# A two-expert-layer kernel: 71 blocks of rows in place of 72, and three of sixteen one-hots on GpSimd

## The reference, cut to what matters

```python
gate_logits = xs @ Wg                                  # 8192 x 8
weights, sel = jax.lax.top_k(gate_logits, 2)
weights = jax.nn.softmax(weights, axis=1)
h = relu(einsum('td,edf->etf', xs, W1) + b1[:, None, :])
out_e = einsum('etf,efd->etd', h, W2) + b2[:, None, :]
out = einsum('tk,tkd->td', weights, out_e[sel, tok[:, None]])
```

## Time and profile before

| | us |
|---|---|
| median of 3 runs | 2251.55 (2251.38 to 2252.23) |
| the profiled execution | 2256.53 |
| its span | 2254.7 |
| ffn1 one-hots | 708.59 to 751.12 |
| ffn2 one-hots | 1763.87 to 1806.42 |
| ffn1 block results, first to last | 782.8 to 1015.6 |

### The profile page before, as it was taken

How to read it: one execution, slowest core, us unless ns; L and a number is a source line. 1 busy time by engine, 2 the same in 40 slices (tenths; PEclk the granted TensorE clock), 3 DMA queues, 4 the chain that set the end, 5 groups by cost and what they waited for, 6 DMA issues and landing times. The chain is left out here.

```text
span 2254.7 us, 51777 instructions
## 1 busy us (share of the span) xinstructions
PE 1673.6 (74%) x16844; PEld 1360.7 (60%) x16844; DVE 1794.9 (80%) x4769; ACT 1480.4 (66%) x3849; POOL 1335.4 (59%) x1497
## 2 busy tenths in 40 slices
PE   5778777787654599993899999999987469997000
PEld 2555555455552388882788888888877258886000
DVE  6999999999878677785899999999957957776221
ACT  5787878788544577771788888888873747775000
POOL 3555556565500355533899999999870045553774
PEclk8888888888756699995999999999985679998555
DMA  1001010010340033331111111111102013333322
GB/s 35 15 15 29 15 29 21 22 29 10 95 146 19 27 81 80 82 72 33 26 29 31 31 30 31 31 31 31 27 8 75 0 49 80 81 82 64 80 77 56
DMA packets 145827, 101.59 MB, mean 45 GB/s; under 512 B 22144, under 2 KB 134688, under 8 KB 145568
## 3 DMA queue, kind: packets, MB, share of 16 engines
q1 hardware_dynamic: 110880, 54.20, 8.7%
q0 software_dynamic: 17408, 35.69, 6.9%
q10 hardware_dynamic: 17280, 8.40, 1.3%
HBM read 53.63 MB, written 35.65 MB: 40 GB/s over the span
## 5 line engine op out<-in xcount | busy, mean ns | idle before, releaser
L1067 POOL DMA_INDIRECT ffn_xs<-normed,ffn_tokeni x288 | 274.2, 952 | 450.6 <-DVE posi L1444 252.5
L1854 POOL TENSOR_TENSOR att_pl<-att_p,att_ph 128x384 f16<-128x384 f32 x512 | 454.6, 916 | 53.6 <-ACT att_ph L2075 45.3
L326 POOL TENSOR_TENSOR sq<-states,qS 128x256 f32<-128x256 f32 x256 | 243.0, 949 | 236.9 <-DVE states L754 235.0
L573 ACT ACTIVATE decayed<-states,alpha 128x64 f32<-128x64 f32 x1024 | 272.1, 336 | 107.4 <-DVE states L754 105.4
L1274 ACT ACTIVATE ffn_h<-bank,b_cols 128x256 f32<-128x256 f32 x576 | 226.1, 474 | 129.6 <-PE bank L1162 118.7
L2182 DVE TENSOR_REDUCE att_mx<-bank 128x3 f32<-128x384 f32 x512 | 279.6, 551 | 36.3 <-PE bank L1911 32.5
L2072 ACT ACTIVATE att_p<-bank 128x384 f32<-128x384 f32 x512 | 252.0, 492 | 57.1 <-PE bank L1948 54.3
L403 PEld LDWEIGHTS bank<-sq,ident 128*128 128x128 f32 x1024 | 225.6, 251 | 46.0 <-issue 26.7
L2075 ACT ACTIVATE att_ph<-bank 128x384 f16<-128x384 f32 x512 | 253.3, 495 | 0.0
L403 PE MATMUL bank<-sq,ident 128*128 128x128 f32 x1024 | 247.7, 413 | 3.3 <-POOL sq L326 3.3
L1175 PE MATMUL bank<-w_h,ffn_hh 128*128 x1152 | 226.0, 224 | 12.7 <-issue 3.8
(11 more groups left out here) (340 smaller groups left out, 5057.8 us busy)
## 6 DMA issues: line engine op xcount, KB each, us to landing
slots<-ffn_ys SPq DMA_DIRECT2D x144, 128.0 KB
normed<-ffn_xn ACTq DMA_DIRECT2D x32, 256.0 KB, 2.3
att_qz<-att_qp SPq DMA_DIRECT2D x256, 32.0 KB
ffn_xs<-normed,ffn_tokeni POOLq DMA_INDIRECT x288
xin<-in_x SPq DMA_DIRECT2D x64, 64.0 KB, 2.0
xres<-in_x SPq DMA_DIRECT2D x64, 64.0 KB, 2.0
x<-x SPq DMA_DIRECT2D x64, 64.0 KB, 1.8
x_all<-x SPq DMA_DIRECT2D x8, 512.0 KB, 4.8
```

The lines of the kernel that those rows point to most:

```text
L326: nc.gpsimd.tensor_tensor(sq[:, t, :].rearrange("p (h i j) -> p h i j", h=HL, i=D), states[:, t, :].rearrange("p (h i j) -> p h i j", h=HL ...
L573: ins = nc.scalar.activation(decayed[:, 64 * h:64 * h + 64], states[:, (t - 1) % TC, 64 * h:64 * h + 64], ACT.Copy, scale=alpha[p][:, t, h ...
L1067: pool.indirect_dma_start(xs[j % AHEAD][:, r, :], None, A["normed"], bass.IndirectOffsetOnAxis(ap=tokeni[:, BR * j + r:BR * j + r + 1], ax ...
L1854: nc.gpsimd.tensor_tensor(pl[:, h % RP, :], p32[:, h % RP, :], ph[:, h % RP, :], ALU.subtract).then_inc(low_done, 1)
```

## The change

Two edits. First, the number of blocks that are worked off becomes `NJ` = `NB` - 1 = 71; `quads` runs over 71 turns, the last turn of buffer 3 falls away (`turns(3)` is 17), the waits that counted 72 // 4 = 18 turns count `turns(p)`, and the HBM tensor `slots` has 71 x 256 rows. Second, in the one-hot stage ACT's `is_tile` does tile 7 only, and POOL makes the `isa` of tiles 5 and 6 and the `isb` of tile 5. A step's one-hots are then 7 `isb` and 5 `isa` on DVE, 1 `isa` on ACT, 1 `isb` and 2 `isa` on POOL. ACT's L1252 also waits for the new semaphore `pool_onehots`.

```diff
+NJ = NB - 1
...
-ACT_TILES = (6, 7)
+ACT_TILES = (7,)
+POOL_TILES = (5, 6)
+POOL_COLS = (5,)
...
-            for i in range(NB // AHEAD):
-                for p in range(AHEAD):
-                    step(i, p, i % 2)
+            for j in range(NJ):
+                step(j // AHEAD, j % AHEAD, j // AHEAD % 2)
+        def turns(p):
+            return len(range(p, NJ, AHEAD))
...
+            pool.wait_ge(route, R["col"])
+            def onehot(i, p):
+                u = 2 * i + p
+                if u >= OH:
+                    pool.wait_ge(counted, u - OH + 1)
+                for q in POOL_TILES:
+                    t = u * TQ + q
+                    if q in POOL_COLS:
+                        pool.tensor_scalar(isb[u % OH][:, q, :], X.slot_col[:, :], col_of[:, t:t + 1], None, ALU.is_equal)
+                    ins = pool.tensor_scalar(isa[u % OH][:, q, 0, :], X.slot_tile[:, :], tile_of[:, t:t + 1],
+                                             X.nth[:, t:t + 1], ALU.is_equal, ALU.mult)
+                ins.then_inc(pool_onehots, 1)
+            pairs(pool, 2 * NT // TQ, onehot)
...
-            for j in range(NB - AHEAD):
+            for j in range(NJ - AHEAD):
...
-                pe.wait_ge(fetched[p], before + 32 * (i + 1))
+                pe.wait_ge(fetched[p], 32 * (turns(p) * calls + i + 1))
...
+                act.wait_ge(pool_onehots, u + 1)
                 nc.scalar.activation(isa[u % OH][:, :, 1, :], isa[u % OH][:, :, 0, :], ACT.Copy, scale=X.row[:, :]).then_inc(rowed, 1)
...
-                    ins = v.tensor_scalar(isb[u % OH][:, q, :], X.slot_col[:, :], col_of[:, at], None, ALU.is_equal)
-                    if q not in ACT_TILES:
+                    if q not in POOL_COLS:
+                        ins = v.tensor_scalar(isb[u % OH][:, q, :], X.slot_col[:, :], col_of[:, at], None, ALU.is_equal)
+                    if q not in ACT_TILES + POOL_TILES:
...
-    A["slots"] = nc.dram_tensor("slots", (NS, E), F32).ap()
+    A["slots"] = nc.dram_tensor("slots", (NJ * BS, E), F32).ap()
```

More of the change, by code:

```diff
@@ L966, in ffn @@
         stats_seen = sem("stats_seen")
+        pool_onehots = sem("pool_onehots")
         x_part = [sem(f"x_part{k}") for k in range(8)]
@@ L969, in ffn @@
         xn_kept = [sem(f"xn_kept{p}") for p in range(2)]
-        fetched, before = X.fetched, 32 * (NB // AHEAD) * X.calls
+        fetched, calls = X.fetched, X.calls
         X.calls += 1
@@ L1021, in within @@
         def within(i, p, n):
-            return not isinstance(i, int) or AHEAD * i + p + n < NB
+            return not isinstance(i, int) or AHEAD * i + p + n < NJ
         def last_group(i, p):
@@ L1051, in _ @@
             for k in range(AHEAD):
-                sp.wait_ge(kept[k], 16 * (NB // AHEAD))
+                sp.wait_ge(kept[k], 16 * turns(k))
             if dst is None:
@@ L1068, in fetch @@
                         ap=tokeni[:, BR * j + r:BR * j + r + 1], axis=0)).then_inc(fetched[j % AHEAD], 16)
+            pool.wait_ge(route, R["col"])
+            tile_of, col_of = (x[:, :, :].rearrange("p k t -> p (k t)") for x in (tile, col))
+            def onehot(i, p):
[10 more added lines that the diff above has]
+            pairs(pool, 2 * NT // TQ, onehot)
             for p in range(2):
@@ L1082, in _ @@
             for p in range(AHEAD):
-                pool.wait_ge(kept[p], 16 * (NB // AHEAD))
+                pool.wait_ge(kept[p], 16 * turns(p))
             for g in range(NG):
@@ L1193, in _ @@
             quads(pe, step)
-            down(NB // AHEAD - 1, AHEAD - 1, expert(pe, regs, (NB // AHEAD - 1) % 2, AHEAD - 1))
+            last = (NJ - 1) // AHEAD, (NJ - 1) % AHEAD
+            down(*last, expert(pe, regs, last[0] % 2, last[1]))
         @block.scalar
@@ L1491, in _ @@
             quads(dve, step)
-            rows(NB // AHEAD - 1, AHEAD - 1, expert(dve, regs, (NB // AHEAD - 1) % 2, AHEAD - 1))
+            last = (NJ - 1) // AHEAD, (NJ - 1) % AHEAD
+            rows(*last, expert(dve, regs, last[0] % 2, last[1]))
             for g in range(0 if dst is None else NG):
```

## The result

| | before, us | after, us |
|---|---|---|
| median, four runs of each | 2251.62 | 2239.89 |
| ratio, with its 95% interval | | 0.995 (0.9937 to 0.9962) |
| the profiled execution | 2256.53 | 2241.95 |
| one-hot stage (start of `ffn_col` to start of `ffn_past`), ffn1 / ffn2 | 42.8 / 42.9 | 39.8 / 39.8 |
| block results, first to last, ffn1 / ffn2 | 232.8 / 232.4 | 225.3 / 226.7 |

The kernel became 11.7 us faster; 8 us slower was forecast.

What follows compares the result with a forecast made beforehand. DVE, with ACT level, was taken to bound the one-hot stage and PE the blocks. Blocks -6.5 and one-hots +14.4 (POOL's price outweighing DVE's saving) made +8 on the median 2251.55, so 2259.5 us, range 2232 to 2273.

Steps and rivals of the forecast that it cites:

- What bounds the kernel: DVE sets the one-hot stage, with ACT level; PE bounds the block stage; each us of the one-hot stage is the kernel's.
- One block less, -6.5: Block loops of ffn1 and ffn2: one middle block's period goes in each, 3.28 + 3.26 = -6.5 us.
- DVE loses 0.389: One-hot stage: DVE drops one `isb` and one `isa`, step 2.66 to 2.27, giving -12.4 us without a price.
- ACT loses 0.71: One-hot stage: ACT drops one `is_tile`, 0.40 of Abs and 0.31 of Relu, its round going from 2.70 to 1.99.
- POOL's length, 0.35: One-hot stage: a POOL one-hot takes 0.35 us, between 0.31 and 0.47, so three fit in a step at 1.05.
- the second rival: One-hot stage: POOL becomes the bound at 0.92 a one-hot, step 4.44, total 2302; chance 0.12, shared with a higher price.
- The price, 0.79 x 0.35 = 0.28 a one-hot: One-hot stage: each POOL one-hot costs DVE 0.28 us (0.22 to 0.39), step 3.11, turning the term into +14.4 us.
- The share of 0.72 to 0.83: Rows before the change: DVE's loss beside a POOL instruction, as share of POOL's own length; mean 0.79 applied to one-hots.
- the first rival: One-hot stage: POOL's one-hots cost DVE under 0.15 each; 2232.6 at 0, 2242 at 0.10; chance 0.37.

Runs made afterwards that it cites:

- the one-hots alone: Kernel before with only the new one-hot split, still 72 blocks: 2166.96 against 2171.68 us, ratio 0.9975.
- the spare one-hots: Kernel before plus three POOL one-hots a step that nobody reads, DVE and ACT keeping all work: 2179.61 against 2171.68 us, ratio 1.0031.
- the long one: Kernel before plus one spare POOL compare of 128x512 f16 a step, one scalar per partition: 2185.68 against 2172.48 us.
- two tensors on DVE and the spare one-hots: Kernel before with each DVE `isb` a two-tensor compare, plus three spare POOL one-hots a step: 2183.4 us, kernel before 2174.59.
- the spare sums: Kernel before plus three spare POOL two-tensor sums of 128x144 f16 a step: 2189.82 us in one run, kernel before 2174.59.
- The blocks alone: Kernel after with POOL's one-hots given back to DVE and ACT, leaving only the 71 blocks: 2163.82 against 2171.68 us, ratio 0.9961.
- the `isa` alone: Kernel after with POOL's `isb` given back to DVE, so POOL makes two `isa` a step: 2162.75 against 2171.68 us, ratio 0.9957.
- the split with two `isb`: Kernel after with POOL making two `isb` and one `isa` a step: 2248.48 us against 2259.89 for the kernel before, ratio 0.9951.

## Why the prediction was wrong

*What bounds the kernel: right.* DVE set the one-hot stage, and a us of it was a us of the kernel: in the one-hots alone the stages lost 6.3 and the kernel 4.7, in the spare one-hots they gained 7.4 and the kernel 7.9, in the long one 13.6 and 13.2. It was less close in two single runs: 12.1 and 8.8 with two tensors on DVE and the spare one-hots, 18.7 and 15.2 with the spare sums.

*One block less, -6.5: right.* The blocks alone gave -7.9 with 5.6 to 11.5, for two blocks of 2.89. In the first pair of traces the stretch of results shrank more, by 7.5 and 5.7, which is more than a block each, because the results also stood 0.06 and 0.03 closer. This is not the change's doing: with 71 and with 72 blocks they stood 2.89 apart in one series, and in a later trace of the kernel after 228.9 / 70 = 3.27.

*DVE loses 0.389: right. ACT loses 0.71: a little too much.* DVE's undisturbed distances are unchanged, and the step came out as 2.27 plus what POOL costs. ACT's busy time fell by 9.5 us a stage, 0.59 a step; it has 8 us of slack, so this changed nothing.

*POOL's length, 0.35: mis-sized.* It took 0.65 and 0.93, outside 0.31 to 0.47. The forecast took 292 ns of another single-input instruction as the nearest row and left the second rival's 0.92 as a far bound, because "no row is as slow for so few elements". No row had POOL compare at all. The condition of that rival, over 0.76 of mean length, was in fact met (0.83), but its time was not: it held DVE for 0.79 of POOL's round, where the round of 2.46 is simply level with DVE's. It costs little: with the price alone DVE would need 2.45.

*The price, 0.79 x 0.35 = 0.28 a one-hot: this is the step that failed, and it turned the sign.* Measured are 0.077 beside the full DVE load, 0.09 for the `isa` alone, 0.04 in the split with two `isb`, and (2.48 - 2.29) / 3 = 0.065 in the kernel after (39.75 / 16 = 2.48, and 42.85 / 16 - 0.389 = 2.29). As a share of POOL's length this is 5 to 10%. The share of 0.72 to 0.83 was read rightly for what it was, mostly POOL products of two tensors; the failed inference was to carry it to a compare, on the ground that DVE's L2147 had been held too. It had been, but by a POOL memset:

```profile
1033.70 4.50 DVE L2147 TENSOR_SCALAR att_xn<-x_all,att_mv,att_rstd 128x128 f32<-128x128 f32 x2 [3.09 <-ACT att_rstd L2042]
...
1034.22 3.83 POOL L1824 MEMSET att_qz<- 128x4096 f16 x1
```

The pair takes 0.60 at 1042.24, so 3.9 were lost, about the memset's length. So the row does show that a DVE instruction with one tensor can be held, but it says nothing of a POOL compare. With the two-tensor sum on POOL DVE is in fact held to the end of each, and the price is 46% of its length only because one short DVE instruction is let through each time; that is much more than a compare's, and still below the forecast's share. The swap on DVE's side shows that two tensors there do not bring the large price. Which property of POOL's instruction decides is open: the memset reads no tensor and stopped DVE the longest, and the sum differs from the compare in its operation too.

With measured terms the forecast's own sum would have been -6.5 - 12.4 + 96 x 0.065 = -12.7, against -11.7. That is the first rival, "POOL's one-hots slip in between", at the 0.10 or below for which it gave 2242; it had been given 0.37. Of its two reasons both are seen: most of a short POOL one-hot's length stops nothing, and a DVE instruction can make part of a hold good (731.22 in the kernel after, the second hold of the long one).

The Trainium skill (SBUF — State Buffer, Who interferes with whom) has the shared port pair as an exclusive lock that is held for the full instruction. By that, were POOL the first each time, DVE would have stood still for 2.5 us of each step and the stage would have been (2.27 + 2.5) x 16 = 76 us, an estimate; it was 39.8. For this pair of instructions the measurement decides against the rule; for POOL's two-tensor sum, at whose end the DVE instruction beside it ends too, and for the memset of 3.83 that cost 3.9 the trace agrees with it.

## What to carry to other kernels

Before work is moved to GpSimd beside a busy VectorE, put the same instructions there as spare work, with nobody reading them: one such run gives both their length and their price to VectorE. The price does not follow from the length: it was 0.018 to 0.09 us for compares of 0.6 to 1.15 us, 0.195 for a sum of 0.425 and 0.43 for a compare of 1.63. A price that rows show for two-tensor products, or for a memset, must not be carried to compares. When a share of work is moved, the aim is that both engines are level; here the moved work made GpSimd level with VectorE at 2.46 us a step, and only giving some of its long instructions to a third engine with slack brought the rest.

## What was not expected of the hardware

- A compare on GpSimd with 128 f16 elements and one scalar per partition takes 0.64 us, with 144 elements and two such scalars 0.93, with 144 and two fixed numbers 0.72, with 512 elements and one scalar 1.63. A sum of 144 f16 elements with two tensor inputs takes 0.425 and so is the faster form, though the dearer one for VectorE, which gets one instruction done per sum.
- Which engine stands still depends on both kinds. With VectorE's two-tensor compares in the stage, each GpSimd compare cost VectorE 0.018 us and was itself stretched, from 0.93 to 1.15.
- A GpSimd compare of 512 elements holds VectorE twice: for about 0.4 us near its start, which is lost, and for about 0.3 us up to its end, of which VectorE makes all or most good. In between VectorE goes on undisturbed.
- A GpSimd memset of 3.83 us cost a pair of VectorE instructions with one tensor input 3.9 us, about its whole length.
- The same program, the kernel before, took 2252 and 2260 us in two series and 2172 to 2175 in three others, and the series did not all run on one chip. The granted clock of the whole is alike (0.84 to 0.85), and in the blocks it is 1.00 in both; most of the difference is in the blocks, whose results are 3.28 us apart in the one and 2.89 in the other (2 x 72 x 0.39 = 56 of about 80 us). Its cause was not looked for; it is larger than the whole change, so only times of one series were compared.
